# Latent attention of a two-layer perceiver block: a longer opening, and each slot's values step put ahead of its energies

## What is computed

```python
x = layer_norm(image_embeds, ln1_g, ln1_b)      # context, 32 x 256 x 256
l = layer_norm(latents, ln2_g, ln2_b)           # the residual's rows, normed twice
q = l @ Wq
k, v = split(concat([x, l], axis=1) @ Wkv)      # 320 keys and values for each batch
w = softmax(einsum('bhqd,bhkd->bhqk', q * scale, k * scale))
return (einsum('bhqk,bhkd->bhqd', w, v) -> rows) @ Wo
```

## Time and profile before

| what | value |
|---|---|
| median of 3 runs | 2005.67 us (2005.25 to 2007.06) |
| the profiled execution | 2004.79 us, span 2003.1 us |
| granted TensorE clock, mean | 0.996 |
| PE busy | 1946.3 us, 97% of the span |
| PEld busy | 1697.0 us, 85% |
| DVE busy | 1232.0 us, 62% |
| ACT busy | 1110.5 us, 55% |
| POOL busy | 601.6 us, 30% |
| latent attention | 0 to about 768 us of the span |

### The profile page before, as it was taken

How to read it: one execution, slowest core, us unless ns; L and a number is a source line. 1 busy time by engine, 2 the same in 40 slices (tenths; PEclk the granted TensorE clock), 3 DMA queues, 4 the chain that set the end, 5 groups by cost and what they waited for, 6 DMA issues and landing times.

```text
span 2003.1 us, 43992 instructions
## 1 busy us (share of the span) xinstructions
PE 1946.3 (97%) x17307; PEld 1697.0 (85%) x17307; DVE 1232.0 (62%) x3579; ACT 1110.5 (55%) x2432; POOL 601.6 (30%) x652
## 2 busy tenths in 40 slices
PE   6899999999999998998999999999999999999998
PEld 6798989888898885677788888789999999999998
DVE  6666677776767665676578998537748623243212
ACT  5566666666666663332487876544444444444443
POOL 1311141111112101322212212344444444444444
PEclk9999999999999999999999999999999999999999
DMA  5556555555545542000311110101010110101000
GB/s 191 152 171 190 168 163 156 163 154 148 165 146 159 153 125 74 1 1 1 88 37 34 34 34 2 44 1 64 1 43 1 43 43 1 43 1 43 1 12 32
DMA packets 100333, 154.21 MB, mean 77 GB/s; under 512 B 12897, under 2 KB 78753, under 8 KB 100001
## 3 DMA queue, kind: packets, MB, share of 16 engines
q1 hardware_dynamic: 100128, 151.41, 24.6%
HBM read 103.73 MB, written 43.45 MB: 73 GB/s over the span
## 4 chain that ended last, share of the span: by engine, by line
PE 46%; DVE 2%; ACT 2%; issue 1%; POOL 0%; POOLq 0%; DVEq 0%; ACTq 0%
PE bank L83 21%; PE bank L1132 18%; PE bank L1053 2%; PE bank L1040 1%; PE bank L1068 1%; ACT att_p L1238 1%; PE bank L1098 1%; PE bank L1009 1%; ACT att_pt L1243 1%; PE bank L1079 0%; POOL right_h L963 0%; DVE dec_room L140 0%; ACT att_kt L1230 0%; PE bank L1091 0%; DVE att_vz L1385 0%
## 5 line engine op out<-in xcount | busy, mean ns | idle before, releaser
L963 POOL TENSOR_TENSOR right_h<-right_hr,right_h 128x512 fp32r<-128x512 f32 x256 | 341.7, 1335 | 417.5 <-ACT right_hr L1285 417.5
L1284 ACT ACTIVATE right_h<-bank,dec_b 128x512 fp32r<-128x512 f32 x256 | 176.3, 688 | 389.5 <-PE bank L83 364.9
L83 PE MATMUL bank<-lat_kv_t,lat_qk 128*128 128x320 f32 x1536 | 255.2, 315 | 10.3 <-issue 7.2
L83 PEld LDWEIGHTS bank<-lat_kv_t,lat_qk 128*128 128x128 f32 x1536 | 229.1, 189 | 22.7 <-issue 7.6
L83 PE MATMUL bank<-lat_wv,lat_kv_t 128*128 128x512 f32 x960 | 242.5, 393 | 1.5 <-DVE lat_qk L2446 1.5
L2312 ACT ACTIVATE lat_p<-bank,lat_neg_max 128x320 f32<-128x320 f32 x256 | 134.4, 526 | 164.0 <-DVE lat_neg_max L2451 164.0
L83 PEld LDWEIGHTS bank<-lat_wv,lat_kv_t 128*128 128x128 f32 x960 | 175.4, 188 | 32.3 <-DVE lat_qk L2446 2.4
L83 PE MATMUL bank<-dec_xt,dec_lo 128*128 128x512 f32 x512 | 200.6, 392 | 0.0
L1285 ACT ACTIVATE right_hr<-bank,dec_b 128x512 f32<-128x512 f32 x256 | 174.5, 682 | 0.0
L2471 DVE STREAM_TRANSPOSE lat_pb<-lat_p 128x640 f32<-128x640 f32 x126 | 106.3, 844 | 107.5 <-DMA lat_turns<-lat_pb 66.2
L2451 DVE TENSOR_REDUCE lat_neg_max<-bank 128x1 f32<-128x320 f32 x256 | 120.9, 484 | 74.2 <-PE bank L83 70.2
(11 more groups left out here) (332 smaller groups left out, 3813.6 us busy)
## 6 DMA issues: line engine op xcount, KB each, us to landing
lat_turns<-lat_pb SPq DMA_DIRECT2D x63, 640.0 KB, 3.3
lat_pt<-lat_turns SPq DMA_DIRECT2D x252, 160.0 KB, 3.1
raw_w<-in_L_ffn_W SPq DMA_DIRECT2D x16, 1024.0 KB, 6.5
lat_ctx_raw<-in_ctx SPq DMA_DIRECT2D x16, 512.0 KB, 5.0
right_ctx_raw<-in_ctx_turned SPq DMA_DIRECT2D x16, 512.0 KB, 3.7
lat_kv_f<-in_ctx_turned SPq DMA_DIRECT2D x15, 512.0 KB, 4.2
lat_ctx_raw<-gate_rows SPq DMA_DIRECT2D x15, 512.0 KB, 4.5
lat_kv_t<-lat_lt SPq DMA_DIRECT2D x32, 128.0 KB, 4.1
```

The lines of the kernel that those rows point to most:

```text
L83: mm = pe.matmul(out, lhs(a, k), rhs(b, k), start=first and k == 0 and n == 0, stop=last and k == KD - 1 and n == 2)
L963: pool.tensor_tensor(h[:, g % 2, 1, :], hr[:, g % 2, :], h[:, g % 2, 0, :].bitcast(F32), ALU.subtract).then_inc(h_lo, 1)
L1284: act.activation(h[:, n % 2, 0, :], h_bank[n % 2][:, :], ACT.Relu, bias=bias).then_inc(h_hi, 1)
```

## The change

In the opening, TensorE and ScalarE take the first latent values and the first values of pair 0 behind the first query keys; VectorE takes the statistics of pair 1's context, its columns' turn and the statistics of all latents ahead of the first split of the query keys. Pair 0's slots lose this work and otherwise get the same places as in the other pairs. SyncE spreads pair 1's columns ahead of the first slot; for other pairs the four small writes, the first weights out, the broadcast, and the weights back now follow each other in this order. In every slot TensorE computes the values before the energies, ScalarE copies them out before the exponentials, and scales right behind these. The bank order is the old one, but for pair 0's moved steps. The wait for the context's split moves from energies to values.

```diff
-            if s in (1, 5):
+            if s == 5 or s == 1 and pair:
                 steps.append(("l", pair, s // 4))
...
-            steps = [("v", pair, s)] + extras(pair, s)
+            steps = ([("v", pair, s)] if pair or s else []) + extras(pair, s)
...
         opening = [("m", 0, 0), ("m", 1, 0), ("t", 0, 0), ("t", 0, 1), ("q", 0, 0), ("q", 0, 1), ("q", 0, 2), ("q", 0, 3),
-                   ("g", 0, 0)]
+                   ("g", 0, 0), ("l", 0, 0), ("v", 0, 0)]
...
+            def spread_back(i):
                 sp.wait_ge(cols_out, 64 * i)
                 sp.dma_start(ctx_raw[:, :, :].rearrange("p t d -> p (t d)"),
                              k.scratch[i].rearrange("j p -> (j p)").partition_broadcast(P)).then_inc(cols_in, 16)
-            def weights_turned(n):
+            def weights_out(n):
...
+            def weights_back(n):
                 sp.wait_ge(p_out, 16 * (n + 1))
...
+            spread(1)
+            spread_back(1)
...
-                if 1 <= i < NT - 1:
+                spreads = 1 <= i < NT - 1
+                if spreads:
                     spread(i + 1)
                 for n in range(NU // 2):
-                    if i < NT - 1 or n < NU // 2 - 1:
-                        weights_turned(NU // 2 * i + n)
-                    if i == 0 and n == 0:
-                        spread(1)
+                    turned = i < NT - 1 or n < NU // 2 - 1
+                    if turned:
+                        weights_out(NU // 2 * i + n)
+                    if n == 0 and spreads:
+                        spread_back(i + 1)
+                    if turned:
+                        weights_back(NU // 2 * i + n)
...
             def values(c, off, a):
-                if a == 0 and 2 * c + off == 0:
-                    pe.wait_ge(w_lo[2], 1)
+                if a == 0:
+                    pe.wait_ge(t_lo, 2 * (2 * c + off) + 2)
...
             def slot(c, off, s, first, last):      # TensorE
+                here = 2 * c + off
+                if here or s:
+                    values(c, off, s)
                 energies(c, off, s)
...
             def slot(c, off, s, first, last):      # ScalarE
                 here = 2 * c + off
+                if here or s:
+                    values(c, off, s)
                 weights_of(c, off, s, 0)
                 weights_of(c, off, s, 1)
+                normalise(c, off, s)
                 for kind, pair, a in others(here, s):
                     to = off + pair - here
                     if kind == "g":
-                        if s == (4 if here else 6) and here + 1 < NT:
+                        if s == 4 and here + 1 < NT:
...
-                    if kind == "v":
-                        normalise(c, off, s)
...
             def slot(c, off, s, first, last):      # VectorE
-                if i == 0:
-                    if s == 0:
-                        dve.wait_ge(x_in[1], 16)
-                    if 2 <= s < 6:
-                        split_last_weight(s - 2)
-                    for t in range(3 * s + 2, min(3 * s + 5, NT)):
-                        norm_x.row(dve, x_sb[:, t, :], t - 2)
-                    if s == 5:
-                        norm_x.finish(dve, 0)
-                    if s in (0, 1):
-                        context_rows(1, (2 * s, 2 * s + 1))
+                if i == 0 and 2 <= s < 6:
+                    split_last_weight(s - 2)
...
-                if more and s == (6 if i else 7):
+                if more and s == 6:
                     for kd in range(KD):
                         context_split(c, off + 1, kd)
...
             split_weight(2)
+            context_rows(1, range(4))
+            norm_c.finish(dve, norm_c.steps)
+            dve.wait_ge(x_in[1], 16)
+            for t in range(2, 6):
+                norm_x.row(dve, x_sb[:, t, :], t - 2)
+            turn_columns(1)
+            for t in range(6, NT):
+                norm_x.row(dve, x_sb[:, t, :], t - 2)
+            norm_x.finish(dve, 0)
             for h in (1, 0):
                 query_keys(0, 0, 0, h)
```

More of the change, by code:

```diff
@@ L2218, in slot @@
             def slot(c, off, s, first, last):
+                here = 2 * c + off
+                if here or s:
+                    values(c, off, s)
                 energies(c, off, s)
-                here = 2 * c + off
                 for kind, pair, a in others(here, s):
                     to = off + pair - here
+                    if kind == "v":
+                        continue
                     if kind == "g" and not (first and off == 0 and s < 4):
@@ L2236, in _ @@
             for kind, pair, a in opening:
-                if (kind, a) == ("q", 0):
-                    pe.wait_ge(w_lo[0], 1)
+                if kind in "ql" and a == 0:
+                    pe.wait_ge(w_lo[{"q": 0, "l": 2}[kind]], 1)
                 if (kind, a) == ("g", 0):
@@ L2345, in slot @@
                             output(c, back, hp // 2)
-                    if kind in do and not (last and to >= 2):
-                        if here == 0 and kind == "l" and a == 0:
-                            act.wait_ge(made, 9)
+                    if kind in do and kind != "v" and not (last and to >= 2):
                         do[kind](c, to, a)
-                    if kind == "v":
-                        normalise(c, off, s)
                 if here == 0 and s == 1:
@@ L2372, in _ @@
                     split_weight(2)
+                if kind == "l":
+                    act.wait_ge(made, 9)
                 if kind in do:
@@ L2510, in slot @@
                     k.ahead.norm.row(dve, x_sb[:, i - 1, :], i - 1)
-                if i == 0:
-                    if s == 0:
-                        dve.wait_ge(x_in[1], 16)
-                    if 2 <= s < 6:
-                        split_last_weight(s - 2)
-                    for t in range(3 * s + 2, min(3 * s + 5, NT)):
-                        norm_x.row(dve, x_sb[:, t, :], t - 2)
-                    if s == 5:
-                        norm_x.finish(dve, 0)
-                    if s in (0, 1):
-                        context_rows(1, (2 * s, 2 * s + 1))
+                if i == 0 and 2 <= s < 6:
+                    split_last_weight(s - 2)
                 if i >= 1 and more and s == 0:
                     context_rows(i + 1, (2, 3))
-                if more and s == (0 if i else 1):
                     norm_c.finish(dve, (i + 1) * norm_c.steps)
-                if more and s == (1 if i else 2):
+                if i >= 1 and more and s == 1:
                     turn_columns(i + 1)
-                if s == (6 if i else 7) and off == 0 and not last:
+                if s == 6 and off == 0 and not last:
                     if i == 0:
```

## The result

The changed kernel takes **2015.37 us** (median, 2014.79 to 2018.34) against 2006.22 us (2005.25 to 2007.06) for the kernel before on the same chip: ratio 1.0049, 95% interval 1.0031 to 1.0066. It is slower, by about as much as was forecast (2013 us). Its profiled execution took 2014.79 us with a span of 2013.1, 10.0 more than the span of before.

A forecast was written before the change was run, and what follows sets the result against it. TensorE, busy 97% of the span, was taken as the bound, so only its standing or low-clock time counts. 2004.8 - 9.3 - 4.9 + 22.3 = 2012.9, forecast as 2013 us, range 2004 to 2020.

The forecast's parts named there:

- Part 3: Every slot, values ahead of energies: shared banks lose 1.76 us of cover, so new waits cost 22.3 us in sum.
- (a) to (d): Four kinds of slot where values wait for ScalarE's readout of latent values, latents or queries; costs 13.2, 2.4, 2.9, 2.1 us.
- (a): Latent values, queries, then values, at 14 places: values wait for ScalarE's latent copies, 0.94 us each, 13.2 us.
- (b): Pair 15, slot 5: no queries follow the latent values, so values are due sooner; cost 2.4 us.
- (e): Keys of slot 6 in even pairs, then values of slot 0: the split frees the bank late, cost 1.0 us.
- (f): Pair 3, slot 1, already held by a transfer behind the feed-forward weights: 0.7 us more.
- Part 1: Hole at pair 1: context statistics in the opening and its split in slot 6 remove TensorE's stand, gain 9.3 us.
- Part 2: SyncE's order: weights sent out before the broadcast end nine waits before the output projection, gain 4.9 us.
- Rival 1: Readouts come in time, so Part 3 costs nothing: 1990.6 us; chance 0.22, in full or by more than half.
- Rival 2: The opening idles TensorE for 3.5 us into the lower clock, price about 1.8 us: 2015 us; chance 0.08.
- Rivals 3 and 4: Weights still land late, 2018 to 2024 us, chance 0.08; pair 1's hole stays through another link, 2020 to 2022, chance 0.05.

The follow-up runs named there:

- Experiment 1: Changed kernel with the old slot order on TensorE and ScalarE (energies, then values), new opening and SyncE order kept: 1992.27 us, ratio 0.9931.
- experiment 4: Changed kernel with ScalarE's latent-value copies moved ahead of its scaling: 2004.0 us, ratio 0.9988 to the kernel before.
- experiment 5: Changed kernel with ScalarE's two latent-value copies cut into eight of 128 columns: 2020.4 us.
- experiment 6: The old-slot-order kernel (new opening, new SyncE order) with ScalarE's two latent-value copies cut into eight of 128 columns: 1993.11 us.
- experiment 2: Kernel before with only SyncE's new order (weights out, then broadcast, then weights back): 1999.98 us, ratio 0.9973.
- experiment 3: Kernel before with only the new slot order, old opening and old SyncE order: 2036.04 us, ratio 1.015.
- experiment 8: Changed kernel with ScalarE's split of the last weight moved from slot 1 of pair 0 into the opening: 2016.66 us.
- experiment 10: Old slot order, new opening, early last-weight split, with ten latents' statistics rows and their finish moved back into pair 0's slots 0 to 4: 1987.75 us, ratio 0.9903.
- experiment 11: Changed kernel with ten latents' statistics rows and their finish moved from the opening back into pair 0's slots 0 to 4: 2012.2 us, ratio 1.003.
- experiment 7: Changed kernel with the new order on TensorE alone, ScalarE again copying values out behind the exponentials: 2035.18 us, ratio 1.0139.
- experiment 9: Old-slot-order kernel (new opening, new SyncE order) with ScalarE's split of the last weight moved from slot 1 into the opening: 1991.57 us.

## Why the prediction was right, point by point

- **What bounds the kernel.** TensorE's standing time was the right quantity: nearly all of the shift between the two traces (all but 0.1 us of the 10.0) is one of its waits or a clock period.
- **Part 3, (a) to (d)**, the bulk of the sum, came out within 0.3 us each, with the mechanism as told: two banks in strict turn, 1.76 us of energies gone from between the steps, ScalarE's readout behind a scaling that waits for VectorE. Experiment 1 takes the whole price away (23.1 us), experiment 4 takes seven eighths of (a)'s price (0.83 of 0.94 a place) and (b)'s first 0.83, experiments 5 and 6 put a known step on the readout and find it in the time under one order and not under the other. That the weighing switch costs nothing extra was right: 0.09 us beyond the spacing of the matmuls ahead of it, before and after.
- **(e) was undersized** (1.5 for 1.0), and **(f) had the wrong sign.** I let a wait for a transfer in pair 3 grow by 0.7; it vanished (-1.6), and a like one came in pair 11 (1.02 us at 546.88). Pair 3's wait doesn't follow the change: it is gone in experiment 2 (SyncE's order alone) and in experiment 3 (slot order alone) as well, and it was there again (+1.4 us) with experiment 8's edit, which is far from it. There SyncE reads those weights back 5.6 us after it sent them out, in the changed kernel 3.7. It should have stood as 1.5 us either way. Pair 11's wait does come with the new slot order (0.2 to 1.2 us, experiment 1), and part 3 left it out.
- **Part 1 was 2.0 us too large.** The failing step is "it comes back by slot 4, since the 1.64 us wait there came of VectorE's rows, which are gone". The weighing of slot 4 still comes 0.98 us later than in the kernel before, that of slot 6 1.37 later. The loader waits 0.63 and 0.26 us for `lat_v` in slots 3 and 4 and 0.86 us for `lat_qk` at 57.66. Ahead of that one VectorE's turn of slot 4 had waited for a transfer:

```profile
55.79 0.84 DVE L2486 STREAM_TRANSPOSE lat_pb<-lat_p 128x640 f32<-128x640 f32 x1 [2.27 <-DMA lat_turns<-lat_pb]
```

  The same turn waited 1.58 us in the kernel before, so this wait grew; the 3.40 us of slot 6's turn are gone. What I missed is that the loss of the opening isn't paid back by itself; experiments 10 and 11 show that it was real (3.9 and 3.2 us) and came of the opening's rows. Two slips in the working matter less: its own terms give 69.83 for m, not 69.95 (71.89 was measured), and at the energies of slot 2 the new kernel is ahead by one values step alone, since the one before had its latent step done by then too.
- **Part 2 was 0.8 us too small.** I subtracted 0.27 us at each of nine places as time the loader has anyway. The shifts give 5.66 in all: 0.18 a place would have done.
- **Rival 1 (the readouts come in time)** is refuted: the copies end at M+5.33, not before M+4.57, because the scaling ahead of them waits for VectorE's reciprocal, as the argument against the rival said. Experiment 4 shows that the copies have to be put ahead of the scaling for that.
- **Rival 2 (the lower clock in the opening)** did not happen in this trace (1.00 granted from 30 to 40 us, after a stand of the loader of 3.6 us). That was partly luck: in five of the eight traces with the whole new opening it did happen (experiments 1, 4, 5, 6 and 7, behind stands of the loader of 3.3 to 4.2 us), for 1.4 us in experiment 5 and 2.1 in experiment 4. The price I gave it (about 1.8 us) did come at a place that I hadn't named: the start of the next stage. TensorE, changed kernel and then the kernel before:

```profile
774.73 0.95 PE L2176 MATMUL bank<-lat_wo,lat_at 128*128 128x256 f32 x6 [1.01 <-DVE lat_at L2492]
777.61 4.49 PE L434 MATMUL bank<-ahead_wkv,ident 128*128 128x512 f32 x6 [1.93 <-PEq L2607]
```

```profile
766.39 0.95 PE L2166 MATMUL bank<-lat_wo,lat_at 128*128 128x256 f32 x6 [1.01 <-DVE lat_at L2477]
769.27 2.81 PE L434 MATMUL bank<-ahead_wkv,ident 128*128 128x512 f32 x6 [1.93 <-PEq L2593]
```

  The same six matmuls behind the same stand of 1.93 us took 4.49 us with the clock at 1.2 GHz for most of the time and 2.81 at 2.4. So of the 10.0 us between the spans 8.3 are the change's steps and 1.65 are this. Among all 13 traces only those of the kernel before and of experiment 8 got through that start at full clock, so it is the trace of before that was lucky. The closeness of 2013 to 2015 is partly chance: the miss of 2.0 in part 1, this 1.65 and 0.8 from (a) and (e) are set against 0.8 more gained in part 2, 1.3 in (f) and small change.
- **Rivals 3 and 4** fell with the first two views: no wait is left before L2176, and no hole near 70 us.

## What to carry to other kernels

When steps share banks in strict turn, list for each bank the time at which the next user asks for it and the time at which its reader is done, for every step that is moved, its own bank too; the order is free as long as all of these differences stay positive. A negative one was paid in full where nothing else stood close by (experiment 5); where many came together they covered one another in part (experiment 7: 35.0 us of waits for `lat_v`, 8.3 fewer for `lat_v_l`, 20.0 us of time). Here moving a step of 1.76 us out of the gap cost 0.94, 0.4 and 0.3 us in places that had shown no wait at all before. Move the reader with the step, and put a copy that frees a bank ahead of work that waits for another engine. Work taken out of a loop to fill a hole belongs only as far into the opening as the hole asks: the context's part removed it, the ten other rows only delayed the first slot.

## What the runs showed of the hardware

TensorE's granted clock fell to 1.2 GHz behind stands of very different length, and the length alone didn't tell whether it would. (The stands here are gaps between matmuls; the loader's are 0.2 to 0.4 us longer.) After the 1.93 us at the start of the next stage the changed kernel ran at 1.2 GHz and the kernel before did not. The 2.07 us in pair 15 were followed by 1.2 GHz in experiments 7, 8 and 11 and not in the changed kernel; in experiment 8 the next stage then started at full clock and gave 1.6 us back, in the two others the clock fell there again. In the opening the clock was low around a stand of 1.87 us in experiment 2, 2.87 in experiment 6 and 3.65 in experiment 4, while 3.54 in experiment 8 left it at full. Where such a period could be read by itself it cost 1.4 to 2.1 us. That is as much as experiments 8 and 9 were to find, so small edits were compared by the shifts ahead of such a period and not by the time alone. The Trainium skill (TensorE: Matmul & The Clock Gate, Part 1) says that the counter behind the gate runs on its own, so that the moment of a change depends on where the work happens to lie against it. One stand with two outcomes agrees with that; no run here moved the work against the counter on purpose.

Eight copies of 64 x 128 took 0.33 us more than two of 64 x 512 (1.49 against 1.16): six more instructions at 0.055 each, where I had expected some 0.2.
